# Mixer and fp4 FFN on one core: the gate projection z in eight half-length pieces, paired transpositions, decodes moved

## The chip, the cores and the metric

One core of a Trainium2 chip runs the whole kernel in one launch. The metric is the device time of one execution in microseconds. Names used below: PE is TensorE, DVE VectorE, ACT ScalarE, POOL GpSimd, SP SyncE, whose queue issues all transfers.

## The reference, cut to what matters

`x` holds 8 batches of 512 tokens of 512 features. Each layer is followed by a residual sum and a layer norm.

```python
def mixer(u, ...):                     # Mamba2-like
    z, xBC, dt = split(u @ in_proj_w.T, [1024, 1024 + 256])     # z, x: 1024; B, C: 128 each; dt: 64 heads
    x, B, C = split(silu(causal_conv4(xBC) + conv_b))
    dt = softplus(dt + dt_bias)
    y = chunked_scan(x, dt, -exp(A_log), B, C) + x * D          # chunks of 64 tokens, 64 heads of 16
    yg = y * silu(z)
    return (yg * rsqrt(mean(yg**2) + EPS) * norm_weight) @ out_proj_w.T
def ffn(x, ...):                       # weights packed as fp4 with a scale per group of 128
    h = silu(x @ w_gate.T) * (x @ w_up.T)                       # 1408 wide
    y = h @ w_down.T
    return y / sqrt(mean(y**2) + EPS)
x = layernorm(x + mixer(x)); x = layernorm(x + ffn(x))
```

## The kernel before, in words

The kernel has two phases, first the mixer for all batches, then the FFN for all. Every engine runs its own instruction stream in an order written out by hand, and they meet at semaphores (`wait_ge`, and `need`, which leaves out waits that hold anyway).

**Mixer.** After a prologue that splits `in_proj_w` into a high and a low fp16 part and projects batch 0, there is one stage `body` for each of batches 0 to 6 and a stage `last` for batch 7. A stage scans batch b in 32 slots n, chunk c = n // 4 and head group g = n % 4, while it projects batch b+1 in between: a tile of 128 columns by 512 tokens is 12 fp16 matmuls (3 passes of high and low parts over 4 row blocks) into one of two PSUM banks `ps_in`. `BODY_USES` gives the slot of each tile (dt, B, C, x0 to x7), of the fp32 out-projection of a quarter of the tokens (o0 to o3, 16 matmuls) and of its sum of squares (q0 to q3). `TAIL` and `HEAD` list what stands between slot 31 and the next scan's slot 0: I call this the border. T' is the end of q3 at a border, where the tail of one batch is done and the head of the next begins.

**A slot.** PE forms exponents in `ps_d` (`exponents`, L843), ACT takes their exponential into one of four buffers `decay` (`exp_group`, L1089), DVE multiplies two groups at a time by `gb` (`mixing`, L1381), PE applies the result within the chunk (L855). POOL scales x into `xend` (`to_end`, L1710), from which PE forms the chunk's new state (L880); `from_before` (L867) adds the older state. Once a chunk, POOL begins y with x times D (`skip_term`, L1724), and three aux groups a0, a1, a2 of PE and ACT prepare it: two of four transpositions each of `xs` (L828, taken to `xpad` by ACT, L1072), one of the product of B and C and B transposed (L831, L834, taken to `gb`, L1076). Since a `decay` buffer serves both `mixing` and `to_end`, ACT's exponentials trail both, and PE's trail ACT's:

```python
            def exp_group(b, n):
                act.wait_ge(d_full, b * SLOTS + n + 1)
                need(act, m_done, b * (SLOTS // 2) + n // 2 - 1)
                need(act, xe_done, b * SLOTS + n - 3)
```

`need(pe, e_done, b * SLOTS + n - 1)` in `exponents` is the other one. Exponential and Silu are in different tables of ACT: each change between them is an ACT_TABLE_LOAD.

**Scale of u.** fp16 splitting wants the largest |u| of a batch: DVE `measure_u` (L1259), POOL's PARTITION_ALL_REDUCE (L1700), DVE `scale_u` (L1268 to L1274), then `split_hi` on ACT (L998) and `split_lo` on DVE (L1280), and dt's matmuls (L774) are the first to read the result. `measure_u` for the batch after next stands at the border.

**Decodes.** Six units per batch of FFN weights are unpacked by DVE (`decode`, three instructions for gate/up, five for down), loaded and stored through SP.

**FFN.** Eight periods of 88 units. A full one has 176 gate/up and 132 down matmuls, fp16 128x512, down one batch behind. At four units of a period `turn` transposes a quarter of the next batch's x: four fp32 transpositions on PE (L889), ACT's high part (L1116), DVE's low part (L1485).

Of the kernel before, what the change touches and what calls it, by code (L numbers as in the profile page):

```python
# [86 lines left out]
IN_COL |= {f"z{i}": NH + 2 * NS + DI + i * P for i in range(CT)}  # L87
# [110 lines left out]
def build(nc, u_t, u_tok, w_in_t, conv_w, conv_b, dt_bias, a_log, d_skip, norm_w, w_out_t,  # L198
# [3 lines left out]
    with ctx:  # L202
# [258 lines left out]
        TURN_AT = [12 + TILE_UNITS * i for i in range(KT)]  # L461
        TILE_MMS = 3 * FT
# [1467 lines left out]
```

## Time and profile before

| | before |
|---|---|
| median of 3 runs | 1707.49 us (1706.34 to 1711.44) |
| profiled execution: time, span | 1713.24 us, 1711.1 us |
| busy PE, DVE, POOL, ACT | 92%, 76%, 64%, 53% |
| FFN's first gate/up matmul | 1140.63 us after the span's start |
| first e0 of each batch | 103.19, 223.39, 355.62, 488.82, 622.03, 755.23, 888.44, 1021.63 us |
| full FFN period | 68.22 us |

The profile is of one execution: the span is what the trace covers, 2.1 us less than that execution's time. An engine's busy share is an average over both phases. Distances between equal points of successive batches (e0 is the first `exponents` of one) are more telling than the shares.

### The profile page before, as it was taken

The numbers are of one execution on the slowest core, as the hardware profiler recorded it, in microseconds if no ns is written. First come the engines' busy times: TensorE is split into PE (matmuls) and PEld (weight loads), VectorE is DVE, ScalarE is ACT, GpSimd is POOL, SyncE is SP. The second block draws the span as 40 slices with busy tenths as digits, with TensorE's granted clock in tenths as the row PEclk, the third lists the DMA queues.
The fourth block names the chain that finished last, engine by engine and source line by source line (L and its number), as shares of the span: only waits on it lengthen the run. The fifth ranks groups of instructions, "written<-read, shape, count | busy, mean of one in ns | idle before, by whom it ended". The sixth has DMA issues, their size and how long they took to land.

```text
span 1711.1 us, 39013 instructions
## 1 busy us (share of the span) xinstructions
PE 1568.0 (92%) x14272; PEld 769.4 (45%) x14272; DVE 1301.6 (76%) x1994; ACT 906.6 (53%) x1585; POOL 1093.1 (64%) x1085
## 2 busy tenths in 40 slices
PE   2789899899999989999999997879999999999998
PEld 1245445445445445445445444433444444444443
DVE  6769859968868868868877877957777767777774
ACT  2663454364364455445545444328676756666662
POOL 0349739739729738827837845748776766767773
PEclk9899999999999999999999998989999999999999
DMA  7031161151152142133124128321010111111101
GB/s 238 8 99 31 29 142 31 29 121 50 27 115 60 23 101 64 29 79 93 27 63 111 25 55 245 51 67 38 13 62 26 62 51 34 53 44 43 35 28 62
DMA packets 214763, 109.80 MB, mean 64 GB/s; under 512 B 133876, under 2 KB 185776, under 8 KB 214576
## 3 DMA queue, kind: packets, MB, share of 16 engines
q1 hardware_dynamic: 214576, 107.37, 24.0%
q8 instruction: 109, 1.79, 0.4%
q14 instruction: 78, 0.64, 0.1%
HBM read 80.57 MB, written 26.76 MB: 63 GB/s over the span
## 4 chain that ended last, share of the span: by engine, by line
PE 69%; DVE 13%; issue 6%; ACT 6%; POOL 2%; DMA 1%; SPq 1%; DVEq 0%; ACTq 0%; POOLq 0%
PE ps_in L781 17%; PE ps_in L941 8%; PE ps_in L803 8%; PE ps_yd L956 7%; PE ps_yo L956 7%; PE ps_s L941 4%; PE ps_t L941 4%; DVE pre L1293 4%; PE ps_yd L855 3%; PE ps_yo L867 2%; PE ps_d L843 2%; PE ps_t L828 2%; PE ps_s L880 2%; ACT decay L1089 1%; ACT xpad L1072 1%
## 5 line engine op out<-in xcount | busy, mean ns | idle before, releaser
L1089 ACT ACTIVATE decay<-ps_d 128x512 f32<-128x512 f32 x256 | 149.0, 592 | 233.3 <-PE ps_d L843 179.5
L781 PE MATMUL ps_in<-u_hi,w_hi 128*128 128x512 f16 x576 | 224.3, 389 | 38.2 <-DVE pre L1293 15.9
L1710 POOL TENSOR_TENSOR xend<-xpad,decay 128x256 f32<-128x256 f32 x256 | 205.2, 822 | 69.1 <-PE ps_yo L880 47.5
L803 PE MATMUL ps_in<-w_out,zg 128*128 128x512 f32 x512 | 229.3, 601 | 0.9
L781 PE MATMUL ps_in<-u_hi,w_lo 128*128 128x512 f16 x576 | 223.6, 388 | 0.0
L781 PE MATMUL ps_in<-u_lo,w_hi 128*128 128x512 f16 x576 | 223.5, 388 | 0.0
L1818 POOL TENSOR_TENSOR gate_sum<-gate_sum,gate_part 128x512 f32<-128x512 f32 x88 | 142.1, 1615 | 104.0 <-DVE gate_part L1631 103.6
L1381 DVE TENSOR_TENSOR mix<-decay,gb 128x1024 f32<-128x1024 f32 x128 | 188.9, 1476 | 17.9 <-ACT decay L1089 16.0
L1293 DVE SCALAR_TENSOR_TENSOR pre<-ps_in,cws,pre 128x511 f32<-128x511 f32 (+2 forms) x240 | 178.9, 746 | 28.0 <-ACT pre L1029 22.3
L803 PEld LDWEIGHTS ps_in<-w_out,zg 128*128 128x128 f32 x512 | 95.5, 192 | 131.6 <-issue 131.6
L1029 ACT ACTIVATE pre<-ps_in,cb,cws 128x512 f32<-128x512 f32 x80 | 62.2, 778 | 164.2 <-PE ps_in L781 164.2
L941 PE MATMUL ps_in<-xt_hi,gu_w 128*128 128x512 f16 x352 | 134.6, 382 | 6.7 <-DVE gate_sum L1631 2.2
L941 PE MATMUL ps_in<-xt_lo,gu_w 128*128 128x512 f16 x352 | 134.4, 382 | 0.0
L1818 POOL TENSOR_TENSOR up_sum<-up_sum,up_part 128x512 f32<-128x512 f32 x88 | 112.9, 1283 | 15.9 <-DVE up_part L1631 15.5
L1724 POOL TENSOR_TENSOR y<-xs,dskip 128x512 f32<-128x512 f32 x64 | 81.2, 1269 | 58.2 <-issue 49.2
L781 PEld LDWEIGHTS ps_in<-u_hi,w_hi 128*128 128x128 f16 x576 | 57.3, 100 | 119.2 <-DVE res L1450 17.9
L843 PE MATMUL ps_d<-rhs_d,lhs_d 94*128 94x512 bf16 x256 | 102.3, 400 | 3.7 <-DMA lhs_d<-ld_dram 3.2
L1826 POOL TENSOR_TENSOR h_lo<-hf,h_hi 128x512 f16<-128x512 f32 x88 | 103.1, 1172 | 0.3 <-ACT h_hi L1222 0.3
L855 PE MATMUL ps_yd<-mix,xpad 128*32 128x64 f32 x4096 | 87.9, 229 | 14.9 <-DVE mix L1381 13.7
L1631 DVE SCALAR_TENSOR_TENSOR gate_part<-ps_in,gs,gate_part 128x512 f32<-128x512 f32 x88 | 66.0, 750 | 46.6 <-ACT gate_part L1208 36.7
L1072 ACT ACTIVATE xpad<-ps_t 64x256 f32<-64x256 f32 x256 | 95.0, 371 | 7.6 <-PE ps_t L828 6.1
L1408 DVE TENSOR_TENSOR yoff<-ps_yo,ebc 128x512 f32<-128x512 f32 x56 | 38.6, 689 | 76.8 <-PE ps_yo L867 73.4
(194 smaller groups left out, 3742.3 us busy)
## 6 DMA issues: line engine op xcount, KB each, us to landing
ebc<-e_dram SPq DMA_DIRECT2D x256, 64.0 KB, 2.8
u<-u_t SPq DMA_DIRECT2D x9, 1024.0 KB, 5.6
res<-u_tok SPq DMA_DIRECT2D x32, 256.0 KB, 3.4
x_dram<-res SPq DMA_DIRECT2D x32, 256.0 KB, 2.3
xa<-x_dram SPq DMA_DIRECT2D x8, 1024.0 KB, 6.0
xr<-x_dram SPq DMA_DIRECT2D x32, 256.0 KB, 2.6
out<-xr SPq DMA_DIRECT2D x32, 256.0 KB, 2.0
fw_words<-gu_words SPq DMA_DIRECT2D x32, 176.0 KB, 4.0
```

The lines of the kernel that those rows point to most:

```text
L781: last = mm(ps_in[bk][:, :], w[:, k, col:col + P], u[:, k, :], start=(k == 0 and j == 0), stop=(k == KT - 1 and j == 2))
L803: last = mm(ps_in[bk][:, :], zg[:, k, tt * P:(tt + 1) * P], w_out[:, k, :], start=(k == 0), stop=(k == CT - 1))
L843: mm(ps_d[n % 2][:, :].rearrange("p (k t) -> p k t", k=CT), lhs_d[0:94, c % 2, g, :], rhs_d[0:94, c % 2, g * CT:(g + 1) * CT, :], start=Tr ...
L855: last = mm(ps_yd[strip * 32:(strip + 1) * 32, tile * CH:(tile + 1) * CH], xpad[:, c % 2, g * CT + e, :], mix[:, g, e, :], start=True, sto ...
L941: last = mm(ps_gu[u % len(ps_gu)][:, :], gu_w[:, g, col:col + P], x[p.par][:, g, :], start=(j == 0), stop=(j == 1))
L956: last = mm(ps_n[tt % 2][:, :], h[par][:, k, tt * P:(tt + 1) * P], w[:, k, :], start=(step == 0), stop=(step == TILE_MMS - 1))
L1072: last = ac(xpad[rows, c % 2, 16 * use:16 * use + 16, h2 * HD:(h2 + 1) * HD], src, ACT.Copy)
L1089: ac(decay[:, n % NG, :, :].rearrange("p a b -> p (a b)"), ps_d[n % 2][:, :], ACT.Exp).then_inc(e_done, 1)
L1293: ins = v.scalar_tensor_tensor(pre[:, m, d:L], ps_in[bk][:, 0:L - d], cws[:, m, k:k + 1], pre[:, m, d:L], ALU.mult, ALU.add)
L1381: v.tensor_tensor(mix[:, g:g + 2, :, :].rearrange("p g e t -> p (g e) t"), decay[:, g:g + 2, :, :].rearrange("p g e t -> p (g e) t"), gb[: ...
L1710: g_.tensor_tensor(xend[:, pairs, :], xpad[:, c % 2, pairs, :], decay[:, g, :, CH - 1:CH].broadcast_to([P, CT, 2 * HD]), ALU.mult).then_in ...
L1818: g_.tensor_tensor(to[:, buf, :], to[:, buf, :], part[:, buf, :], ALU.add).then_inc(part_done, 1)
```

## The change

It does five things. **z** becomes eight pieces Z0 to Z7, each two column tiles by half of the tokens: 24 matmuls of 256 columns instead of 2 x 12 of 512 per pair of tiles. Z0, Z1, Z2 stand at slots 22, 24, 30 of the scan before, Z3 in place of z0, Z4 and Z5 in the border, Z6 and Z7 at slots 0 and 1. ACT takes them raw, and one Silu for each half of the tokens (`silu_z`, 128x2048) follows, at the border and at slot 12; a semaphore `z_done` tells the gates. **Transpositions** go in pairs: `xs` lies chunk by chunk, a0 is four transpositions of 128x128 with four copies to `xpad`, and with B doubled a1 is one matmul and one transposition. **Order**: `scale_u` moves from slot 0 to the end of slot 1, where it waits until Z6 and Z7 are taken; the splits, dt, B and C move a slot later; `measure_u` moves behind the last `norm_tile_end`, `take_out` ahead of `use_in`. **Decodes** of units 2 and 3 move ahead of o3's taking, units 4 and 5 to slots 2 and 3 of the next scan. **FFN**: for periods 2 to 7, x is transposed by transfers: ACT and DVE write the high and the low fp16 part (`high_half`, and `low_half` likewise on DVE, 128x512 each), SP issues eight transposing transfers of 128 KB per period, and PE waits for them at the next period's start (`xt_in`).

```diff
-DT_SLOT = {7: 0, 10: 1, 13: 2, 18: 3, 20: 4}
-SPLIT_SLOT = {1: (0, 1), 2: (2, 3)}
+DT_SLOT = {8: 0, 10: 1, 13: 2, 18: 3, 20: 4}
+SILU_Z = 12
+SPLIT_SLOT = {2: (0, 1), 3: (2, 3)}
...
-HEAD = ["a0", "z1", "z2", "e0", "a1", "e1", "z3", "a2", "e2", "z4", "z5", "z6", "z7"]
-PRO_ORDER = ["dt", "B", "C", "x0", "x1", "x2", "x3", "x4", "z0", "x5", "z1", "x6", "z2"]
-TAIL = {"pro": ["x7", "z3", "z4", "a0", "z5", "z6", "z7", "e0", "a1", "e1", "a2", "e2"], "body": ["x6", "x7", "z0", "o3", "q3"] + HEAD, "last": ["o3", "q3"]}
-AUX_ORDER = (0, 2, 1)
-NA = len(AUX_ORDER)
+HEAD = ["a0", "e0", "Z4", "a1", "e1", "Z5", "e2"]
+PRO_ORDER = ["dt", "B", "C", "x0", "x1", "x2", "x3", "x4", "Z0", "x5", "Z1", "x6", "Z4"]
+TAIL = {"pro": ["x7", "Z5", "Z2", "a0", "Z3", "e0", "a1", "e1", "e2"], "body": ["x6", "x7", "Z3", "o3", "q3"] + HEAD, "last": ["o3", "q3"]}
+NA = 2
+SILUS = 4
...
-BODY_USES = [(4, "dt"), (5, "B"), (7, "C"), (9, "x0"), (11, "x1"), (12, "o0"), (13, "q0"), (17, "x2"), (19, "x3"),
-             (20, "o1"), (21, "q1"), (25, "x4"), (27, "x5"), (28, "o2"), (29, "q2")]
-LAST_USES = [(12, "o0"), (13, "q0"), (20, "o1"), (21, "q1"), (28, "o2"), (29, "q2")]
+BODY_USES = [(0, "Z6"), (1, "Z7"), (5, "dt"), (6, "B"), (8, "C"), (9, "x0"), (11, "x1"), (12, "o0"), (13, "q0"), (17, "x2"),
+             (19, "x3"), (20, "o1"), (21, "q1"), (22, "Z0"), (24, "Z1"), (25, "x4"), (27, "x5"), (28, "o2"), (29, "q2"), (30, "Z2")]
+LAST_USES = [(0, "Z6"), (1, "Z7"), (12, "o0"), (13, "q0"), (20, "o1"), (21, "q1"), (28, "o2"), (29, "q2")]
...
-    turned = names.index("q2") + 1 if "q2" in names else len(uses)
-    return [(i + (i >= turned)) % 2 for i in range(len(uses))]
+    return [(i + sum(n in ("q1", "q2") for n in names[:i])) % 2 for i in range(len(names))]
...
-                     "last": {n: [(n // 4, n % 4)] for n in range(24)}}
-        DECODE_LATE = {"body": [2, 3, 4, 5], "last": []}
+                     "last": {n: [(n // 4 - 1, n % 4)] for n in range(4, 28)}}
+        DECODE_LATE = {"body": [2, 3], "last": []}
+        DECODE_NEXT = {2: 4, 3: 5}
...
+            def turn(f, par):
+                need(sp, gu_full, (f - 1) * UNITS)
+                settled(sp)
+                for t in range(TT):
+                    sp.wait_ge(half_hi, (f - 2) * TT + t + 1)
+                    settled(sp)
+                    sp.dma_start_transpose(xt_hi[par][:, :, t * P:(t + 1) * P], xh16[:, t, :]).then_inc(xt_in, 16)
+                    sp.wait_ge(half_lo, (f - 2) * TT + t + 1)
+                    settled(sp)
+                    sp.dma_start_transpose(xt_lo[par][:, :, t * P:(t + 1) * P], xl16[:, t, :]).then_inc(xt_in, 16)
...
+                passes = [(w_hi, u_hi), (w_hi, u_lo), (w_lo, u_hi)]
+                if name[0] == "Z":
+                    half, pair = divmod(int(name[1]), CT // 2)
+                    t = slice(half * LH, (half + 1) * LH)
+                    for i in range(2):
+                        col = Z_COL + (2 * pair + i) * P
+                        for k in range(KT):
+                            for j, (w, u) in enumerate(passes):
+                                last = mm(ps_in[bk][:, i * LH:(i + 1) * LH], w[:, k, col:col + P], u[:, k, t],
+                                          start=(k == 0 and j == 0), stop=(k == KT - 1 and j == 2))
+                    last.then_inc(in_full[bk], 1)
+                    return
...
             def aux(b, c, at):
 
-                use = AUX_ORDER[at]
                 need(pe, t_free, (b * NC + c) * NA + at)
-                t = slice(c * CH, (c + 1) * CH)
-                if use < 2:
-                    pe.wait_ge(silu_done, (b + 1) * 3)
+                if at == 0:
+                    pe.wait_ge(silu_done, b * SILUS + 2)
                     settled(pe)
-                    for k in range(4):
-                        last = tr(ps_t[0:CH, k * P:(k + 1) * P], xs[:, 4 * use + k, t], ident[:, :])
+                    for k in range(CT // 2):
+                        last = tr(ps_t[:, k * P:(k + 1) * P], xs[:, c, 2 * k * CH:2 * (k + 1) * CH], ident[:, :])
                 else:
-                    for h2 in range(2):
-                        mm(ps_t[h2 * CH:(h2 + 1) * CH, 0:CH], bc[:, 0, t], bc[:, 1, t], start=True, stop=True,
-                           tile_position=(0, h2 * CH))
-                    for h2 in range(2):
-                        last = mm(ps_t[h2 * CH:(h2 + 1) * CH, CH:CH + NS], bc[:, 0, t], ident[:, :],
-                                  start=True, stop=True, tile_position=(0, h2 * CH))
+                    pe.wait_ge(silu_done, (b + 1) * SILUS)
+                    settled(pe)
+                    mm(ps_t[:, 0:CH], b2[:, c, :], cc[:, c, :], start=True, stop=True)
+                    last = tr(ps_t[:, CH:CH + NS], b2[:, c, :], ident[:, :])
                 last.then_inc(t_full, 1)
...
             def take_z(st, name):
                 bk, _, full = st.bank(name)
                 act.wait_ge(in_full[bk], full)
...
-                if st.kind == "body" and name == "z0":
-                    ob, _, ofull = st.bank("o3")
+                if st.kind == "body" and name in ("Z0", "Z4"):
+                    ob, _, ofull = st.bank("o1" if name == "Z0" else "o3")
                     act.wait_ge(in_full[ob], ofull)
-                    act.wait_ge(sq_done, (st.scan + 1) * NC)
-                ac(zg[:, int(name[1]), :], ps_in[bk][:, :], ACT.Silu, scale=uundo[:, 0:1]).then_inc(in_free[bk], 1)
+                    act.wait_ge(sq_done, st.scan * NC + (half + 1) * NC // 2)
+                ac(zg[:, 2 * pair:2 * pair + 2, half * LH:(half + 1) * LH], ps_in[bk][:, :].rearrange("p (k t) -> p k t", k=2),
+                   ACT.Identity, scale=uundo[:, 0:1]).then_inc(in_free[bk], 1)
+
+            def silu_z(b, half):
+
+                for bk, count in Stage("last" if b == nb - 1 else "body", b).z_free(half):
+                    act.wait_ge(in_free[bk], count)
+                t = slice(half * LH, (half + 1) * LH)
+                ac(zg[:, :, t], zg[:, :, t], ACT.Silu).then_inc(z_done, 1)
...
             def aux(b, c, at):
...
+                if at == 0:
+                    need(act, yd_done, b * SLOTS + NG * (c - 1))
+                    need(act, xe_done, b * SLOTS + NG * (c - 1))
+                    for odd in range(2):
+                        for h2 in range(2):
+                            src = ps_t[odd * CH:(odd + 1) * CH, :].rearrange("p (k q h d) -> p k q h d", k=CT // 2, h=2, d=HD)
+                            dst = xpad[h2 * CH:(h2 + 1) * CH, c % 2, :, :].rearrange("p (k o q) d -> p k o q d", o=2, q=NG)
+                            last = ac(dst[:, :, odd, :, h2 * HD:(h2 + 1) * HD], src[:, :, :, h2, :], ACT.Copy)
...
-                    if n == 0 and st.proj is not None:
-                        scale_u(st.proj, st.before())
...
-                    if n > 0:
-                        use_in(st, n - 1)
                     for tt in range(TT - 1):
                         if f"o{tt}" in st.at(n - NORM_AT):
                             take_out(st, tt)
+                    if n > 0:
+                        use_in(st, n - 1)
                     if st.proj is not None:
-                        if n == 5:
+                        if n == 6:
                             dt_first(st)
                         if n in DT_SLOT:
                             dt_second(st.proj, DT_SLOT[n])
                     for k, part in DECODE_AT[st.kind].get(n, []):
                         decode(b, k, part)
+                    if b > 0 and n in DECODE_NEXT:
+                        for part in range(4):
+                            decode(b - 1, DECODE_NEXT[n], part)
+                    if n == 1 and st.proj is not None:
+                        scale_u(st.proj, st)
...
                 for tt in range(TT - 1):
                     norm_tile_end(st, tt)
-                use_in(st, SLOTS, "o")
-                if st.proj is not None:
-                    measure_u(b + 2)
-                norm_tile_end(st, TT - 1)
                 for k in DECODE_LATE[st.kind]:
                     for part in range(4):
                         decode(b, k, part)
+                use_in(st, SLOTS, "o")
+                norm_tile_end(st, TT - 1)
+                if st.proj is not None:
+                    measure_u(b + 2)
...
+            def high_half(f, t):
+                act.wait_ge(xa_in, 16 * (f + 1))
+                need(act, xt_in, (f - 2) * XT_IN)
+                ac(xh16[:, t, :], xa[:, t, :], ACT.Copy, scale=1024.0).then_inc(half_hi, 1)
```

DVE's stream at the border, before, from `measure_u` on (rows of sixteen decode instructions left out but the last; `mix` is `mixing`, `utmp` the beginning of `scale_u`, `cws` its end):

```order
L1259 TENSOR_REDUCE umax<-u 128x1
L1465 TENSOR_SCALAR res<-res,mv,rstd 128x512
...
L1372 TENSOR_TENSOR fw_lo<-fw_w,fw_hi 128x352
L1381 TENSOR_TENSOR mix<-decay,gb 128x1024
L1268 TENSOR_SCALAR utmp<-umax_all 128x1
...
L1274 TENSOR_SCALAR cws<-cw,uundo 128x40
L1381 TENSOR_TENSOR mix<-decay,gb 128x1024
L1280 SCALAR_TENSOR_TENSOR u_lo<-u,uscale,u_hi 128x512 x4
L1381 TENSOR_TENSOR mix<-decay,gb 128x1024
L1415 TENSOR_TENSOR y<-ps_yd,y 128x512
```

The same place of the changed kernel (`fw_words` to `fw_lo` is a decode of five instructions):

```order
L1535 TENSOR_SCALAR res<-res,mv,rstd 128x512
L1330 TENSOR_REDUCE umax<-u 128x1
L1452 TENSOR_TENSOR mix<-decay,gb 128x1024 x2
L1339 TENSOR_SCALAR utmp<-umax_all 128x1
...
L1351 SCALAR_TENSOR_TENSOR u_lo<-u,uscale,u_hi 128x512 x2
L1430 TENSOR_SCALAR fw_words<-fw_words,to_top 128x352
...
L1443 TENSOR_TENSOR fw_lo<-fw_mag,fw_hi 128x352
L1452 TENSOR_TENSOR mix<-decay,gb 128x1024
L1351 SCALAR_TENSOR_TENSOR u_lo<-u,uscale,u_hi 128x512 x2
```

The reduction has gone behind the last norm, the scale behind two multiplications, and a decode stands between the two halves of the split.

ACT's stream around slot 0, before (`zg` is the taking of a z tile):

```order
L1053 ACTIVATE zg<-ps_in,uundo 128x512 x5
L1089 ACT_TABLE_LOAD
L1089 ACTIVATE decay<-ps_d 128x512
L1072 ACTIVATE xpad<-ps_t 64x16x16 x2
L998 ACTIVATE u_hi<-u,uscale 128x512 x2
L1089 ACTIVATE decay<-ps_d 128x512
```

And in the changed kernel:

```order
L1154 ACTIVATE decay<-ps_d 128x512 x2
L1137 ACTIVATE xpad<-ps_t 64x4x4x16 x4
L1109 ACTIVATE zg<-ps_in,uundo 128x2x256
L1154 ACTIVATE decay<-ps_d 128x512
L1141 ACTIVATE gb<-ps_t 128x192
L1109 ACTIVATE zg<-ps_in,uundo 128x2x256
L1048 ACTIVATE u_hi<-u,uscale 128x512 x2
L1154 ACTIVATE decay<-ps_d 128x512
```

The takings of z are now among the exponentials, two of them behind the exponentials that wait for POOL, and no table is loaded between.

## Rows read from the trace of the kernel before

**Rows 1.** Windows: us, busy us of the engines (instructions), PE clock, DMA share, GB/s.

```profile
616.13:649.34 33.21, 29.78 (x229) 15.02 (x228) 22.08 (x40) 20.53 (x37) 8.86 (x12) 0.95 0.59 125
649.34:749.33 99.99, 95.37 (x1235) 48.66 (x1234) 82.58 (x116) 43.91 (x81) 78.61 (x83) 0.98 0.17 45
...
1331.37:1399.59 68.22, 68.22 (x325) 32.00 (x324) 52.09 (x88) 46.47 (x79) 48.33 (x42) 1.00 0.13 44
```

**Rows 2.** Chain of waits, one batch: start, us, piece.

```profile
520.69 0.44 PE ps_t L828 x4
...
521.35 2.59 PE ps_in L781 x12
```

**Rows 3.** Timeline of POOL at a border: start, us, instruction, idle before.

```profile
627.29 0.40 POOL L1700 PARTITION_ALL_REDUCE umax_all<-umax  x1 [7.62 <-ACT xpad L1072]
634.74 1.03 POOL L1724 TENSOR_TENSOR y<-xs,dskip 128x512 f32<-128x512 f32 x1 [7.05 <-issue]
635.74 1.79 POOL L1710 TENSOR_TENSOR xend<-xpad,decay 128x256 f32<-128x256 f32 x3
```

**Rows 4.** Waits of POOL: what for, us in total, times, longest.

```profile
POOL y L1724 <- issue: 49.2, 7, 7.2
```

**Rows 5.** Timeline of DVE at the same border.

```profile
616.17 0.16 DVE L1441 TENSOR_SCALAR msv<-ps_yo 128x1 f32<-128x1 f32 x1 [2.50 <-PE ps_yo L791]
...
618.97 2.29 DVE L1259 TENSOR_REDUCE umax<-u 128x1 f32<-128x2048 f32 x1
...
626.66 0.40 DVE L1359 TENSOR_SCALAR fw_words<-fw_words,to_top 128x352 int32<-128x352 int32 x1 [2.81 <-DMA fw_scale<-dn_scales]
...
628.48 0.53 DVE L1372 TENSOR_TENSOR fw_lo<-fw_w,fw_hi 128x352 f16<-128x352 f32 x1
...
642.02 3.52 DVE L1280 SCALAR_TENSOR_TENSOR u_lo<-u,uscale,u_hi 128x512 f16<-128x512 f32 x4
...
645.46 1.21 DVE L1381 TENSOR_TENSOR mix<-decay,gb 128x1024 f32<-128x1024 f32 x1
646.59 0.68 DVE L1415 TENSOR_TENSOR y<-ps_yd,y 128x512 f32<-128x512 f32 x1
647.20 0.69 DVE L1393 COPY state<-ps_s 128x512 f32<-128x512 f32 x1
```

**Rows 6.** Timeline of PE at the same border.

```profile
641.01 0.48 PE L831 MATMUL ps_t<-bc 128*64 128x64 f32 x4 [2.46 <-ACT xpad L1072]
...
648.85 0.34 PE L831 MATMUL ps_t<-bc 128*64 128x64 f32 x4
...
649.34 0.39 PE L781 MATMUL ps_in<-u_hi,w_hi 128*128 128x512 f16 x1
```

**Rows 7.** Timeline of ACT: at the border, and at slot 12.

```profile
638.42 1.28 ACT L1089 ACT_TABLE_LOAD   x1
...
677.83 0.60 ACT L1089 ACTIVATE decay<-ps_d 128x512 f32<-128x512 f32 x1 [7.54 <-PE ps_d L843]
```

**Rows 8.** Lines by form, ACT's Silu: busy and mean, idle before.

```profile
L1042 ACT ACTIVATE xs<-pre 128x2048 f32<-128x2048 f32 x16 | 29.6, 1894 | 0.0
```

**Rows 9.** Timelines of DVE and PE at slots 21 to 25.

```profile
706.70 0.15 DVE L1441 TENSOR_SCALAR msv<-ps_in 128x1 f32<-128x1 f32 x1
...
711.43 0.74 DVE L1450 SCALAR_TENSOR_TENSOR res<-ps_in,rinv,res 128x512 f32<-128x512 f32 x1
...
712.23 0.39 PE L781 MATMUL ps_in<-u_hi,w_hi 128*128 128x512 f16 x1 [1.81 <-DVE res L1450]
```

**Rows 10.** Timeline of PE in the last batch's scan.

```profile
1047.82 0.37 PE L867 MATMUL ps_yo<-bc,state 128*32 128x64 f32 x12
```

**Rows 11.** Lines by form, a weight load of 128 columns.

```profile
L956 PEld LDWEIGHTS ps_yd<-dn_lo,h_hi 128*128 128x128 f16 x176 | 17.3, 98 | 20.9 <-issue 0.3
```

**Rows 12.** DMA issues: times, KB each, us to landing.

```profile
xa<-x_dram SPq DMA_DIRECT2D x8, 1024.0 KB, 6.0
```

More of the change, by code:

```diff
@@ L86 @@
 IN_COL |= {f"x{i}": NH + 2 * NS + i * P for i in range(CT)}
-IN_COL |= {f"z{i}": NH + 2 * NS + DI + i * P for i in range(CT)}
+Z_COL = NH + 2 * NS + DI
+Z_HALF = [["Z0", "Z1", "Z2", "Z3"], ["Z4", "Z5", "Z6", "Z7"]]
 def need(eng, sem, value):
@@ L129, in before, with z_free @@
         return Stage("pro", 0) if isinstance(self.scan, int) and self.scan == 0 else Stage("body", self.scan - 1)
+    def z_free(self, half):
+        counts = {}
+        for name in Z_HALF[half]:
+            held = self if name in ("Z6", "Z7") else self.before()
+            bk, _, full = held.bank(name)
+            counts[bk] = max(counts.get(bk, 0), full)
+        return sorted(counts.items())
     def last_z(self):
-        found = [self.bank(f"z{i}") for i in (CT - 2, CT - 1)]
+        found = [self.bank(name) for name in ("Z6", "Z7")]
         assert found[0][0] != found[1][0]
@@ L461, in build @@
         TURN_AT = [12 + TILE_UNITS * i for i in range(KT)]
+        HALF_AT = [12 + 6 * t for t in range(TT)]
+        XT_IN = 16 * 2 * TT
         TILE_MMS = 3 * FT
@@ L614, in room_free @@
             def room_free(last):
-                for bk, full in last.before().last_z():
+                for bk, full in last.last_z():
                     sp.wait_ge(in_full[bk], full)
-                sp.wait_ge(silu_done, nb * 3)
+                sp.wait_ge(silu_done, nb * SILUS)
                 sp.wait_ge(u_max, nb + 1)
@@ L742, in ffn @@
                     load_xr(p.d, 1)
+                if p.next and not p.first:
+                    turn(p.f + 1, 1 - p.par)
                 if p.down:
@@ L970, in ffn @@
                             down(p, at)
-                    if p.next and u in TURN_AT:
+                    if p.first and u in TURN_AT:
                         turn(p.f + 1, [TURN_AT.index(u)])
@@ L989, in _, with split_hi @@
             ac = nc.scalar.activation
-            def split_hi(b, before, tiles):
+            def split_hi(b, st, tiles):
                 act.wait_ge(u_scale, (b + 1) * 5)
-                if before is not None:
-                    for bk, count in before.last_z():
+                if st is not None:
+                    for bk, count in st.last_z():
                         act.wait_ge(in_full[bk], count)
@@ L1100, in body @@
                         aux(b, c + 1, g)
+                    if n == SILU_Z:
+                        silu_z(b, 1)
                     if g == 2 and c > 0:
@@ L1103, in body @@
                     use_in(st, n)
-                    if st.proj is not None and n == 6:
+                    if st.proj is not None and n == 7:
                         exp_dt(st.proj)
@@ L1244, in ffn @@
                         squares(d, tt)
-                    if p.next and u - 2 in TURN_AT:
+                    if p.first and u - 2 in TURN_AT:
                         turn(p.f + 1, 1 - p.par, [TURN_AT.index(u - 2)])
+                    if p.next and not p.first and u - 2 in HALF_AT:
+                        high_half(p.f + 1, HALF_AT.index(u - 2))
             act.wait_ge(gs_done, 1)
@@ L1685, in ffn @@
                         normed(d, tt)
-                    if p.next and u - 5 in TURN_AT:
+                    if p.first and u - 5 in TURN_AT:
                         turn(p.f + 1, 1 - p.par, [TURN_AT.index(u - 5)])
+                    if p.next and not p.first and u - 5 in HALF_AT:
+                        low_half(p.f + 1, HALF_AT.index(u - 5))
             periods(dve, ffn)
```

138 lines of the change are left out of this document (77 added, 61 removed).

## The prediction

> **What bounds the kernel now.** I read the page's shares first: PE is busy 92% of the span, so I asked where its 8% of idle time lies and cut one batch of the mixer into two windows [rows 1]. The first runs from T' = 616.13, the end of q3, to the start of tile B at 649.34: 33.21 us with PE busy 29.78. The second, to the next T', is 99.99 us with 95.37 busy. PE sets the pace in both. A full FFN period has PE busy for all of its 68.22 us [rows 1]. So what is taken from PE is worth its length wherever PE isn't made to wait instead, and the reading to make is of the border, where the other engines have their long jobs.
>
> There POOL is the one to watch. DVE's reduction starts at 618.97 and takes 2.29 us [rows 5], so it ends at T' + 5.1. POOL's all-reduce ends at 627.69, 6.4 us later, and its next instruction, `skip_term`, starts at 634.74, after 7.05 us in which it waited for nothing that the profile names [rows 3]. That gap is there 7 times, 49.2 us in all [rows 4]. POOL is thus away from T' + 5.1 to T' + 18.6, 13.5 us, and the first `xend` stands behind it. Before, PE needs nothing of POOL in that time: it has seven z tiles of 2.6 us each [rows 2], 18 us. The 2.46 us that it waits at 641.01 [rows 6] are the first stall.
>
> **The border after, step by step** (T is the new end of q3). DVE: the decodes of units 2 and 3 fill the 2.50 us for which it waited for q3 [rows 5], so they cost nothing. The reduction now stands behind the last norm, whose 0.54 us wait for POOL's root; before, it ran meanwhile. Root ready at T + 3.5, norm to T + 4.1, reduction to T + 6.4: 1.3 us later than before. POOL is back at T + 6.4 + 13.5 = T + 19.9; `skip_term` 1.0 and the first `xend` 0.6 (1.79 for three) [rows 3] end at T + 21.5. ACT's exponential of group 4 waits for that `xend` and ends at T + 22.1.
>
> PE until then has a0 0.44, an exponent group 0.2, Z4 2.6, a1 0.3, e1 0.2, Z5 2.6, two groups 0.4, a0 of chunk 1 0.44, Z6 2.6, group 4 0.2, a1 0.3, Z7 2.6, two applications of `mix` 1.2, group 5 0.2 (2.59 and 0.44 by [rows 2]): 14.3 us. Then it stands before the exponents of group 6, which want group 4's exponential, until T + 22.1. That is a wait of 8 us in the place of z tiles that have gone elsewhere.
>
> Behind it on ACT stand `gb` and the taking of Z7 (0.3 and 0.7 [rows 7]), so Z7 is free at T + 23.1, and `scale_u`, now bound to wait for that, ends 1.25 us later at T + 24.4. The first part of `u_hi` takes 0.7: T + 25.1. DVE then has `u_lo` for two row blocks 1.8 (3.52 for four), unit 4's decode 2.35 (626.66 to 629.01), a `mix` 1.2, the other two 1.8 [rows 5]: T + 32.2. dt's 24 matmuls end 1.4 us later, T + 33.6. DVE's next row is unit 5's decode 2.35, then y 0.7 and two state copies 1.3 [rows 5], so the state is there at T + 36.5; the older state's 0.9 on PE (`from_before`) follow, and B starts at T + 37.6. Before it was 649.34 - 616.13 = T' + 33.2. **+4.4.** A decode costs nothing only where DVE waits; here each stands on the path, and without the two B would start at the later of POOL's and PE's ends, about T + 33.
>
> **From B to slot 18.** The paired transpositions save one group of 0.44 of every chunk [rows 2], and the B and C group falls from 0.49 (648.85 to 649.34 [rows 6]) to about 0.32 (64 + 128 columns, at 0.11 per transposition of 128). 0.6 a chunk is 4.8 a batch, but only the three chunks after the border and before slot 18 pass it on: **-1.8**. Those of the border fall into PE's wait, those of slots 20 to 25 before DVE's.
>
> **Slots 22 to 30.** PE's x4 at 712.23 waits for DVE's `res` of o1, after 1.81 idle; q1's mean square, which frees the bank that Z0 takes, comes at 706.70 [rows 9]. Z0 and Z1 (5.2 us) lie between these, but Z1 needs o1's bank. I put Z0 into the gap, Z1 behind `res`, and gain what the two-ahead banks give x4: +1.3, bounded by 0 (both hidden) and 5.2 - 1.8 = 3.4 (only that idle used). Z2 at slot 30 has no gap: 2.6 by [rows 2], 0.2 for its bank, **+2.8**. Batch in all: 4.4 - 1.8 + 1.3 + 2.8 = **+6.7**.
>
> **What costs nothing.** `silu_z` at slot 12 is 1.9 of Silu [rows 8] and two table loads of 1.28, 4.5 us, in ACT's idle of 7.54 before the exponential at slot 15, while PE has o0 [rows 7]. Without cover it would be up to 4.5 a batch; a 128x2048 Silu of SBUF is the same shape as the row, so I take 1.9. 256-column matmuls: a weight load takes 98 ns [rows 11], a 256-column matmul some 108 (half of 2.59 / 12), so it still hides. The bounds are nothing, and the load wholly exposed (a rival, below). Four copies to `xpad` in the place of four, of the same total, change nothing.
>
> **FFN.** 68.22 - 308 x 0.216 leaves 1.75 us of a period for 16 transpositions. They go in six periods: **-10.5**, if the transfers are in time. ACT's and DVE's halves are of the shapes of what goes. Eight transfers of 128 KB a period must land in about 55 us (the first half is ready about 15 us into a period of 68), 6.9 us each if one follows another; the nearest row lands 1024 KB in 6.0 [rows 12]. No row has a transposing transfer.
>
> The Trainium skill bears on that in "VectorE: DVE Perf Modes", section "The three transpose paths": the transposing path of DMA takes 1309 ns for 128x128 of 16 bits. By that a transfer of four blocks is an estimate of 5.2 us and a period 42 us, and the -10.5 stands; no run shown here has one.
>
> **Sum.** First batch: it has POOL's absence too, but no decodes of a batch before, so I put it at +4 from the same walk. Six more batches 6 x 6.7 = +40.2. Last batch: no projection, so no split and dt; its first `from_before` (1047.82 = T' + 32.1 [rows 10]) comes at about T + 29.5: -3. FFN -10.5. Net **+30.3** on the profiled 1713.2, 1743.5. The median of the runs is 5.7 below the profiled time: **1738**.
>
> **Rivals.**
> (a) POOL is away for only its first half. If the 7.05 us behind the all-reduce are not paid again (or not where `skip_term` is free), POOL is back at T + 12.8 [rows 3], PE never stops at group 6, and B starts 7.1 earlier, T + 30.5, 2.7 before what it was. Batch: -2.7 - 1.8 + 1.3 + 2.8 = -0.4, six times -2.4; the first -3 (+4 less 7.1), the last -5 (it has its own work on PE behind), FFN -10.5: -21, 1687. It decides once POOL's first `xend` ends before T + 14.3. For it: the profile names no cause of the gap. Against it: 7 of 7 times.
> The Trainium skill has in "GPSIMD Engine Reference", section 2.1 "Instruction dispatch", that the first call of freshly loaded code costs some 6 us. The trace has 6.4 ahead of the result, which agrees, and 7.05 again behind it, which would be the loading of the code that was there before; if only the first were such a load, (a) would hold. Chance 0.18.
> (b) PE's stalls are conserved: what waits there were stay as they are, and only PE's work counts. 4.8 x 8 = 38.4 and 10.5 less: 1658. For it: PE is busy 95.4 of 100 us behind the border. Against it: the walk. It decides if the exponents of group 6 don't wait. 0.10.
> (c) Wash: half of +6.7, by smaller waits at the border (POOL's xend in time for one decode less, Z1 hidden): 6 x 2 + 1 - 10.5 = +2.5, 1710. 0.12.
> (d) The transposing transfers are late. At 10 us each, eight take 80 of the 55: +25 in each of six periods, 150 on top of the forecast: 1888. It decides above 6.9 us each. 0.05.
> (e) Weight loads of 256-column matmuls aren't hidden: 64 pieces of 12 more matmuls of 0.1 = +77, 1815. 0.03.
> The forecast has 0.52.
>
> **The numbers.** Own range of the forecast 1722 to 1762: Z1 from 0 to 3.4 in place of 1.3 gives -8 to +13, one decode hidden -14, and the granted clock, 0.95 over the border's window [rows 1], may fall further behind the longer stop, up to +10. The whole range takes in the forecast, (a) with 12 us below it, and (c), 0.82 together, and leaves out (b), (d) and (e): 1675 to 1765. A measurement tells 0.3% (5 us) from no change. Faster: (a) and (b), 0.28. Same 0.12. Slower: the forecast, (d), (e), 0.60.
>
> **What would show it.** The chain of a batch should have POOL's `skip_term` (now about T + 19.9) and PE's exponents of group 6 idle for some 8 us with `decay` as releaser. The distance of two batches' e0 should be 139.9 in place of 133.2; B at T + 37.6; `silu_z` at slot 12 inside ACT's idle time; FFN periods of 66.5 with no PE wait at their start. It would be wrong if POOL's gap behind the all-reduce is gone, if PE doesn't reach group 6 by T + 14.3, or if DVE has its `mix` ready elsewhere than I walked.

## The result, and the profile after

The changed kernel takes 1773.78 us (median of 4 runs, 1769.59 to 1776.51), the kernel before beside it 1706.91. The ratio is 1.0375, 95% interval 1.0351 to 1.0399: slower by 67 us, where 31 were forecast. The direction was right and the size was not; the time lies outside the range. The profiled execution has a span of 1774.7 us against 1711.1, 63.6 more, and all sums below are of spans.

Part 1 of the page of the changed kernel:

```profile
PE 1533.9 (86%) x14368; PEld 825.0 (46%) x14368; DVE 1303.9 (73%) x1994; ACT 942.7 (53%) x1611; POOL 1088.9 (61%) x1085
```

PE has 34 us less to do (1568.0 us before) and is 98 us longer idle. To see where, I take the ends of q0 to q3 of each batch on PE's timeline. T is the end of q3. Means over the six intervals from the first T to the last but one, in us; first is the time to the first T, last from the seventh T to the eighth:

| kernel | T to q0 | q0 to q1 | q1 to q2 | q2 to T | batch | first | last | FFN to end |
|---|---|---|---|---|---|---|---|---|
| before | 62.6 | 24.2 | 27.8 | 18.5 | 133.0 | 217.5 | 122.8 | 570.4 |
| after | 67.3 | 23.3 | 31.5 | 21.6 | 143.6 | 225.1 | 121.8 | 564.0 |

So 6 x 10.6 = 63.5 and 7.6 at the start are lost, 1.0 and 6.4 come back. The windows of one batch (T = 656.71, tile B at 695.96, columns as in [rows 1]) and a full FFN period:

```profile
656.71:695.96 39.25, 24.88 (x316) 18.75 (x315) 20.45 (x35) 16.97 (x35) 10.98 (x14) 0.74 0.53 102
695.96:799.23 103.27, 97.08 (x1171) 53.81 (x1170) 84.89 (x121) 51.63 (x85) 76.01 (x81) 0.98 0.17 45
1331.81:1398.94 67.13, 66.83 (x309) 29.95 (x308) 52.88 (x88) 46.51 (x79) 49.30 (x42) 1.00 0.22 59
```

B starts at T + 39.25, not T' + 33.2 [rows 1], and PE is idle for 14.4 us of it instead of 3.4. The mean granted clock fell from 0.95 to 0.74 there, which is 20 us at the half level (1.2 GHz) in place of 3.4. What holds PE is on the timelines of PE, POOL, ACT and DVE:

```profile
670.31 0.39 PE L890 MATMUL ps_d<-rhs_d,lhs_d 94*128 94x512 bf16 x1
680.39 0.61 PE L890 MATMUL ps_d<-rhs_d,lhs_d 94*128 94x512 bf16 x1 [9.70 <-ACT decay L1154]
680.93 1.08 PE L902 MATMUL ps_yd<-mix,xpad 128*32 128x64 f32 x32
...
690.33 0.42 PE L825 MATMUL ps_in<-u_hi,w_hi 128*64 128x256 f16 x2 [1.41 <-issue]
...
692.65 0.45 PE L825 MATMUL ps_in<-u_hi,w_lo 128*64 128x256 f16 x2
...
751.02 0.28 PE L816 MATMUL ps_in<-u_hi,w_hi 128*128 128x256 f16 x1 [3.16 <-DVE msv L1511]
```

```profile
669.36 0.38 POOL L1781 PARTITION_ALL_REDUCE umax_all<-umax  x1 [9.09 <-issue]
678.00 1.03 POOL L1805 TENSOR_TENSOR y<-xs,dskip 128x512 f32<-128x512 f32 x1 [8.27 <-issue]
679.01 2.38 POOL L1791 TENSOR_TENSOR xend<-xpad,decay 128x256 f32<-128x256 f32 x4
```

```profile
679.74 0.60 ACT L1154 ACTIVATE decay<-ps_d 128x512 f32<-128x512 f32 x1 [12.35 <-POOL xend L1791]
680.24 0.32 ACT L1141 ACTIVATE gb<-ps_t 128x192 f32<-128x192 f32 x1
680.45 0.69 ACT L1109 ACTIVATE zg<-ps_in,uundo 128x512 f32<-128x512 f32 x1
```

```profile
660.76 2.28 DVE L1330 TENSOR_REDUCE umax<-u 128x1 f32<-128x2048 f32 x1
...
681.27 0.15 DVE L1339 TENSOR_SCALAR utmp<-umax_all 128x1 f32<-128x1 f32 x1 [15.14 <-ACT zg L1109]
...
692.33 0.52 DVE L1443 TENSOR_TENSOR fw_lo<-fw_mag,fw_hi 128x352 f16<-128x352 f32 x1
692.77 0.68 DVE L1486 TENSOR_TENSOR y<-ps_yd,y 128x512 f32<-128x512 f32 x1
```

Read them downwards in time: the reduction ends at T + 6.3, the all-reduce at T + 13.0, POOL's next instruction starts 8.27 us later at T + 21.3, the first `xend` lets ACT go on, and PE, which has stood before group 6 since T + 14.0, resumes at T + 23.7. Behind the same exponential ACT takes Z7, DVE scales, splits and decodes. DVE then works without a stop from its first `u_lo` (683.29) to the last of the two state copies (694.65), and PE waits for it at the older state, the last thing ahead of B:

```profile
694.70 1.10 PE L914 MATMUL ps_yo<-cc,state 128*32 128x64 f32 x64 [0.45 <-DVE state L1464]
```

The chain of waits of this batch goes through exactly these pieces (and has Z4 and Z0 as one piece each):

```profile
657.43 2.62 PE ps_in L816 x24
...
669.36 0.38 POOL umax_all L1781
669.73 0.07 POOLq L1805 x2
669.81 8.20 issue
678.00 1.03 POOL y L1805
679.04 0.60 POOL xend L1791
...
751.02 4.46 PE ps_in L816 x24
```

### The profile page after: what moved, and what is told of

It reads as the page before. It is cut to its first block, busy times and chain, and to the rows that moved or that the text cites. A ratio compares the mean times of both kernels' runs of the same rounds, so it can differ in the third digit from the quotient of the medians.

```text
span 1774.7 us, 39351 instructions
## 1 busy us (share of the span) xinstructions
PE 1533.9 (86%) x14368; PEld 825.0 (46%) x14368; DVE 1303.9 (73%) x1994; ACT 942.7 (53%) x1611; POOL 1088.9 (61%) x1085
## 4 chain that ended last, share of the span: by engine, by line
PE 59%; DVE 21%; issue 10%; ACT 6%; POOL 2%; DMA 1%; DVEq 0%; ACTq 0%; SPq 0%; POOLq 0%
PE ps_in L854 9%; PE ps_in L816 8%; PE ps_in L988 7%; PE ps_in L832 7%; PE ps_yd L1003 6%; PE ps_yo L1003 5%; DVE pre L1364 5%; PE ps_t L988 4%; PE ps_s L988 4%; PE ps_yd L902 2%; DVE mix L1452 2%; PE ps_yo L914 2%; PE ps_d L890 2%; PE ps_s L927 1%; DVE u_lo L1351 1%
## 5 line engine op out<-in xcount | busy, mean ns | idle before, releaser
L1791 POOL TENSOR_TENSOR xend<-xpad,decay 128x256 f32<-128x256 f32 x256 | 201.1, 808 | 77.6 <-PE ps_yo L927 41.7
L816 PE MATMUL ps_in<-u_hi,w_hi 128*128 128x256 f16 x512 | 145.6, 284 | 35.2 <-DVE msv L1511 28.2
L890 PE MATMUL ps_d<-rhs_d,lhs_d 94*128 94x512 bf16 x256 | 98.2, 410 | 84.0 <-ACT decay L1154 84.0
L816 PE MATMUL ps_in<-u_lo,w_hi 128*128 128x256 f16 x512 | 145.1, 283 | 0.0
L816 PE MATMUL ps_in<-u_hi,w_lo 128*128 128x256 f16 x512 | 145.0, 283 | 0.0
L832 PE MATMUL ps_in<-u_hi,w_hi 128*128 128x512 f16 x320 | 124.3, 388 | 20.3 <-DVE pre L1364 20.3
L1079 ACT ACTIVATE pre<-ps_in,cb,cws 128x512 f32<-128x512 f32 x80 | 62.2, 778 | 135.8 <-PE ps_in L832 135.8
L832 PE MATMUL ps_in<-u_lo,w_hi 128*128 128x512 f16 x320 | 123.8, 387 | 0.0
L832 PE MATMUL ps_in<-u_hi,w_lo 128*128 128x512 f16 x320 | 123.0, 384 | 0.0
L1109 ACT ACTIVATE zg<-ps_in,uundo 128x512 f32<-128x512 f32 x64 | 43.7, 685 | 122.9 <-PE ps_in L816 122.9
```

What stands on the lines that cost most here:

```text
L816: last = mm(ps_in[bk][:, i * LH:(i + 1) * LH], w[:, k, col:col + P], u[:, k, t], start=(k == 0 and j == 0), stop=(k == KT - 1 and j == 2))
L832: last = mm(ps_in[bk][:, :], w[:, k, col:col + P], u[:, k, :], start=(k == 0 and j == 0), stop=(k == KT - 1 and j == 2))
L890: mm(ps_d[n % 2][:, :].rearrange("p (k t) -> p k t", k=CT), lhs_d[0:94, c % 2, g, :], rhs_d[0:94, c % 2, g * CT:(g + 1) * CT, :], start=Tr ...
L1791: g_.tensor_tensor(xend[:, pairs, :], xpad[:, c % 2, pairs, :], decay[:, g, :, CH - 1:CH].broadcast_to([P, CT, 2 * HD]), ALU.mult).then_in ...
```

## The experiments

The theory (A): POOL's absence around the all-reduce stops PE at group 6, since z tiles no longer cover it, and everything that was hung behind it (the scale, two decodes, the later reduction) stands on one path; Z0 to Z2 cost their length where they went. Its rivals: the pieces, the raw taking or the pairs cost by themselves (B, C), or what was moved was hidden. Ratios are to the kernel before, with their 95% intervals; segments are in us as in the table above. The changed kernel is 64 us (0.0375 of 1710) above the kernel before; where I say how many us come back, it is the difference of two ratios times 1710. Each ratio is known to 2 to 5 us, such a difference to some 5; where it matters I give the difference of the profiled spans beside it.

**e1 and e2: no all-reduce, in the changed kernel and in the one before.** In both kernels one line of POOL:

```diff
-                g_.partition_all_reduce(umax_all[:, :], umax[:, :], P, RMAX).then_inc(u_all, 1)
+                g_.tensor_tensor(umax_all[:, :], umax[:, :], umax[:, :], ALU.mult).then_inc(u_all, 1)
```

> The changed kernel with POOL's all-reduce of umax replaced by one elementwise product, so that the largest |u| is no longer found over the partitions (the scale of u is another one; all else runs as it did). Theory A, POOL's absence around the all-reduce is what PE waits for at the exponents of group 6: POOL's skip_term starts at about T + 7 in place of T + 20.7, group 6 doesn't wait, scale_u starts at about T + 14.6 in place of T + 24.5, so each of the 7 batches with a border is some 9 to 10 us shorter (about 134 in place of 143.6) and the time falls from 1774 to about 1708. Rival B, the pieces of 256 columns, the raw eviction and the pairs themselves are what costs: the all-reduce was beside the path, and the time stays within 10 us of 1774.

> The kernel before with the same replacement. Theory A: before, seven z tiles cover POOL's absence, and scale_u waits for the last z tile and not for the all-reduce, so the time stays within 4 us of 1707. If the all-reduce costs the kernel before as much as the changed one (rival: its price is the same wherever it stands), it falls by some 60 us too.

The kernel then leaves the largest |u| over the partitions out. e1: 1704.83 us, 0.9979 (0.9956 to 1.0002). e2: 1711.1 us, 0.9999 (0.9985 to 1.0014). The same replacement takes 68 us off the changed kernel and none off the one before. T to q0 falls from 67.3 to 55.3, the other segments change by 0.6 at most. POOL's timeline of e1, where T is 622.38:

```profile
628.91 0.98 POOL L1781 TENSOR_TENSOR umax_all<-umax 128x1 f32<-128x1 f32 x1 [2.98 <-DVE umax L1330]
629.85 1.04 POOL L1805 TENSOR_TENSOR y<-xs,dskip 128x512 f32<-128x512 f32 x1
```

Both gaps around the all-reduce are gone, and PE passes group 6 at T + 13.8. PE has no wait there at all. Theory A holds for this place, and rival B, in which the all-reduce was beside the path, is refuted. The 11.3 us that come off a batch are a little more than the 10.6 that the change cost, because the border of e1 is 7.3 us shorter than that of the kernel before, while q1 to T stays 7.4 longer. So two costs stand in the changed kernel at once, PE's stop at the border and the z pieces where they went, and either one taken away alone brings back about the whole loss (e1, e3).

**e3: Z0, Z1, Z2 in the border,** and the first `silu_z` behind them.

```diff
-HEAD = ["a0", "e0", "Z4", "a1", "e1", "Z5", "e2"]
+HEAD = ["a0", "Z0", "Z1", "Z2", "e0", "Z4", "a1", "e1", "Z5", "e2"]
...
-             (19, "x3"), (20, "o1"), (21, "q1"), (22, "Z0"), (24, "Z1"), (25, "x4"), (27, "x5"), (28, "o2"), (29, "q2"), (30, "Z2")]
+             (19, "x3"), (20, "o1"), (21, "q1"), (25, "x4"), (27, "x5"), (28, "o2"), (29, "q2")]
```

> The changed kernel with Z0, Z1, Z2 moved from slots 22, 24, 30 to the border, right behind a0, and the first Silu of z behind them; no other order is changed. Theory A: they fill 7.8 of the 9.7 us for which PE waits at group 6, so the border gets no longer, while the stretch from q1 to q2 goes back from 31.6 to 28 and the one from q2 to T from 21.5 to 18.5: 6.6 us a batch, 46 in all, 1728. If PE did not really have this time free there (rival: the border gets longer by what is put in), the time stays at 1774.

1710.43 us, 0.999 (0.9973 to 1.0007): 66 us are back (62 by the spans), the whole loss, where 46 were expected. T to q0 stays at 67.2, so 7.8 us of matmuls lay free in PE's wait; PE's stop there is down to 1.23 us (0.7 to 2.2 over the seven borders):

```profile
644.08 0.39 PE L890 MATMUL ps_d<-rhs_d,lhs_d 94*128 94x512 bf16 x1 [1.23 <-ACT decay L1154]
```

q2 to T gives 3.1, as expected. q1 to q2 falls to 25.5, below the kernel before (27.8): 2.3 us that I had not counted on, which e12 explains.

**e4: the decodes of units 4 and 5 in the border.** On DVE (SP's loads and stores likewise):

```diff
-        DECODE_NEXT = {2: 4, 3: 5}
+        DECODE_NEXT = {}
...
                     measure_u(b + 2)
+                    for k in (4, 5):
+                        for part in range(4):
+                            decode(b, k, part)
```

> The changed kernel with the decodes of units 4 and 5 behind the reduction of umax in the border, where DVE idles for 15 us, in place of slots 2 and 3. Theory A: both stood on the path from scale_u to tile B (2.35 each), so B comes 4.7 us earlier (T + 34.5 in place of T + 39.2) in six batches: 28 us, 1746. Rival: POOL or ACT sets B and the decodes were hidden: no change.

1740.3 us, 1.0156 (1.0129 to 1.0183): 37 us back (32 by the spans), 28 expected. T to q0 is 62.2, 5.1 less per batch, nothing else moves. Both decodes were on the path.

**e10: the reduction of umax ahead of the last norm.** 

```diff
-                norm_tile_end(st, TT - 1)
                 if st.proj is not None:
                     measure_u(b + 2)
+                norm_tile_end(st, TT - 1)
```

> The changed kernel with only the reduction of umax back ahead of the last norm. Theory A: POOL and all that waits for it come 1.2 us earlier in each of seven borders: skip_term at T + 19.5 in place of 20.7, 142.4 us a batch, 8 us in all, 1765. Rival: DVE's takings or the root on POOL set the border, no change.

1768.32 us, 1.0327 (1.0308 to 1.0345), 8 us back; T to q0 is 66.3, 1.0 less, `skip_term` at T + 19.2 to 20.5. As expected.

**e5: all three.** e3, e4 and e10 together.

> The changed kernel with Z0, Z1, Z2 in the border as in e3, the decodes of units 4 and 5 in the border as in e4, and the reduction of umax ahead of the last norm, where it stood in the kernel before. Theory A: the three terms are on one path and add up: the batch of e3, 134.5, less 5.1 for the decodes and 1.2 for the reduction, 128.2 us a batch against 133.0 of the kernel before, some 1670 in all. Rival: with the z pieces in PE's wait, PE and not POOL sets B, and less than half of the 6.3 comes through: about 1690.

1680.95 us, 0.9822 (0.98 to 0.9844): 30 us faster than the kernel before. A batch takes 129.1 (61.3, 23.3, 26.1, 18.5) where 128.2 were expected, and the time is 11 us above the 1670 expected. By the ratios 95 us are back, and the three by themselves brought 66 + 37 + 8 = 111. Most of that difference is in the way of counting: by the spans it is 98.4 of 62.1 + 31.8 + 7.6 = 101.5, and by the batches 14.6 of 9.1 + 5.1 + 0.9 = 15.1. T to q0 gives all of its 6.0, q1 to q2 is 0.6 longer than in e3. So the three terms do add up, to about 3 us. The clock is no loss of e5 as a whole: its mean granted clock is 0.974, against 0.956, 0.950 and 0.949 in e3, e4 and e10. What the clock costs where PE sets the pace is seen within e5. Two neighbouring batches of e5, by the windows:

```profile
736.55:862.45 125.90, 116.47 (x1486) 69.36 (x1485) 105.72 (x155) 68.47 (x119) 87.76 (x94) 1.00 0.27 69
862.45:991.94 129.49, 120.45 (x1485) 71.82 (x1485) 105.37 (x155) 68.53 (x119) 87.01 (x94) 0.96 0.28 67
```

The same instructions take 3.6 us longer where the granted clock is 0.96 (10.2 us at the half level, 1.2 GHz, in its border; none in the other batch); PE's busy time grows by 4.0.

**e11: e5 without the all-reduce.** The line of e1 in e5.

> The kernel of e5 with the all-reduce replaced as in e1 (the largest |u| is not found over the partitions). In e5 PE reaches group 6 at T + 21.7 and POOL's first xend ends at T + 20.5: POOL is covered again. Theory A: at most 1.5 us a batch are left, 1670 to 1681, against the 69 that the same replacement brought the changed kernel. If POOL's absence had a second effect beside the wait at group 6 (a rival), 20 or more come off.

1684.85 us, 0.9841 (0.9825 to 0.9858), where e5 has 0.9822 (0.98 to 0.9844): nothing comes off, and the time lies above the 1670 to 1681 expected, so not even the 1.5 us a batch that I allowed for are there. PE passes group 6 at T + 21.7 in both (22.1 in one border of e5), though `xend` is ready at T + 14.6 instead of 20.3 to 21.4. Once covered, POOL's 13.5 to 14.6 us cost nothing, as in e2.

**e9: Z0 two slots later.** 

```diff
-             (19, "x3"), (20, "o1"), (21, "q1"), (22, "Z0"), (24, "Z1"), (25, "x4"), (27, "x5"), (28, "o2"), (29, "q2"), (30, "Z2")]
+             (19, "x3"), (20, "o1"), (21, "q1"), (24, "Z0"), (24, "Z1"), (25, "x4"), (27, "x5"), (28, "o2"), (29, "q2"), (30, "Z2")]
```

> The changed kernel with Z0 at slot 24 in place of 22, in front of Z1; nothing else is moved. Theory A says that Z0 costs so much at slot 22 because PE, which works in order, waits there 3.2 us for q1's mean square on DVE with the work of slots 22 and 23 behind it, and then runs Z0 at half the clock (4.5 us for 2.6). Behind that work the wait is gone or short: q1 to q2 falls from 31.5 to 28.5 to 30, 1.5 to 3 us a batch, about 1760. Rival: any 5.2 us of new work between q1 and q2 costs its length, since x4 waits for nothing any more: q1 to q2 stays at 31.5 and the time at 1774.

1766.89 us, 1.0326 (1.0309 to 1.0344), 8 us back. q1 to q2 is 30.3, 1.2 less, just short of what was expected, and 4.8 above e3's. Z0 starts without a wait of its own there and at full clock, but PE's wait has only changed its place:

```profile
743.52 0.65 PE L902 MATMUL ps_yd<-mix,xpad 128*32 128x64 f32 x32 [2.29 <-DVE mix L1452]
749.51 0.28 PE L816 MATMUL ps_in<-u_hi,w_hi 128*128 128x256 f16 x1 [0.79 <-DVE res L1520]
```

PE stands 2.29 us for DVE's `mix`, as it does in e3 without any Z there (2.28), and 0.79 before Z1. So of the 3.16 us before Z0 at slot 22 most was a wait for DVE that is there anyway. The place of Z0 was worth a fifth of the 6.0 us; the rest is that new work between q1 and q2 costs its length.

**e12: the rule of the banks alone, in the kernel before.**

```diff
-    turned = names.index("q2") + 1 if "q2" in names else len(uses)
-    return [(i + (i >= turned)) % 2 for i in range(len(uses))]
+    return [(i + sum(n in ("q1", "q2") for n in names[:i])) % 2 for i in range(len(names))]
```

> The kernel before with the changed rule of the banks alone: the order flips behind q1 too, so x4 at slot 25 takes the bank that q1's mean square frees (706.85) and not the one that the taking of o1 frees (712.17). e8 less e6 and e7 leaves it some 15 us. Theory A: the 1.8 us of idle before x4 and its half-clock stretch (1.7) go, q1 to q2 25.4 in place of 27.8, seven batches: 16 us, 1695. Rival: what follows x4 waits for DVE's taking instead (x5 takes that bank), and little or nothing is left: 1707 to 1711; the 15 us of e8 would then come of the pairs and the banks together.

1696.5 us, 0.9927 (0.9902 to 0.9951), q1 to q2 25.2 in place of 27.8 (the whole batch is 2.3 shorter). x4 no longer has the wait of 1.81 us that it has in [rows 9]:

```profile
701.34 0.55 PE L780 MATMUL ps_in<-u_hi,w_hi 128*128 128x512 f16 x1
```

A part of the change that I had not costed by itself gives 2.6 us between q1 and q2.

**e6, e7, e8: the pairs, the FFN transfers, and both with the banks, in the kernel before.** Their code is that of the change, with z, order and decodes as before. The core of e6 on PE, and of e7 on SP (e8 has both and the edit of e12):

```diff
-                    for k in range(4):
-                        last = tr(ps_t[0:CH, k * P:(k + 1) * P], xs[:, 4 * use + k, t], ident[:, :])
+                    for k in range(CT // 2):
+                        last = tr(ps_t[:, k * P:(k + 1) * P], xs[:, c, 2 * k * CH:2 * (k + 1) * CH], ident[:, :])
...
+                if p.next and not p.first:
+                    turn(p.f + 1, 1 - p.par)
```

> The kernel before with the paired transpositions alone (the layouts of xs, B and C, a0 of four and a1 of two instructions, four copies of ACT to xpad, Silu of x first); z, decodes and FFN as before. Theory A: 0.6 us of PE a chunk comes through where PE sets the pace: 0.9 from q0 to q1, some 3 us a batch, 24 in all, 1687. Rival C, four copies behind one group of transpositions are worse for ACT than two behind two: PE waits for a1 at each chunk and the time is 1707 or more.

> The kernel before with the transposing transfers of the FFN alone. The changed kernel's FFN took 564.1 us from its first matmul to the end against 570.4: 6.4 less, so 1701. The prediction's term was 10.5 (1697). Nothing in the mixer should move: 133.0 a batch.

> The kernel before with the pairs, the FFN transfers and the changed rule of the banks (the order of the two banks flips behind q1 too, so x4 takes the bank that q1 frees and not the one that o1's taking frees). In e3 that rule made q1 to q2 25.45 us in place of 27.8. Theory A: -24 for the pairs, -6.4 for the FFN, -2.35 x 7 = -16 for the banks: about 1661. If the pairs give nothing, 1685.

e6: 1702.96 us, 0.9949 (0.9931 to 0.9967), a batch 131.7, so 1.4 of its 4.8 us of PE come through, and I expected 3 (1687 in all). e7: 1704.97 us, 0.9963 (0.9953 to 0.9974), 133.0 a batch; its FFN takes 562.4 us, 8.0 less than before. e8: 1681.68 us, 0.9826 (0.9808 to 0.9844), 29.8 us; e6, e7 and e12 make 8.7 + 6.3 + 12.5 = 27.5, so the three add up as near as can be told. The 1661 expected is missed mostly by what the pairs didn't give. It is as fast as e5 (1680.95), which has z in pieces of 256 columns. That fits pieces that cost nothing, but does not show it alone: e5 also takes z raw and has the changed order and decodes.

## Why the prediction was wrong, step by step

**The border: mechanism right, +4.4 mis-sized, measured +6.0.** PE was to reach group 6 at T + 14.3 and wait until T + 22.1; it reached it at T + 14.0 and waited until T + 22.6 to 23.7. B was to start at T + 37.6 and starts, over the six borders, at T + 38.9 to 39.7, 39.4 in the mean. Half of the 1.8 missing is POOL: it is away for 14.1 to 15.0 us from the reduction's end to `skip_term`, not 13.5, because the gap behind the all-reduce is 7.2 to 8.3 where [rows 3] had 7.05, and the stretch ahead of it is up to 0.6 longer. `skip_term` is 0.9 late, and DVE's last state copy, which the walk has at T + 36.5, ends at 37.4, 0.9 late too. The other half lies behind the state copies: the older state and an exponent group, 1.1 in the walk, take 1.26 where the granted clock is back at its full level (the border shown) and up to 2.27 where it is still at half (1.2 GHz). I walked at full clock and had "up to +10" for that in the range. What the low clock does before that is beside the path: dt's 24 matmuls take 2.8 us for 1.4 in the border shown (690.33 to 693.10), and end 1.5 us before the state copies. Rival (a) is refuted: both halves of POOL's absence are paid each time. Rival (b) too, since group 6 waits.

**The decodes: right.** 4.7 by the walk, 5.1 by e4. The reduction behind the norm: 1.3 by the walk, 1.0 by e10.

**`silu_z` at slot 12: right.** It and its two table loads take 4.5 us, and ACT is idle for 2.2 more before the exponential behind them.

**From B to q1: right within 0.5.** T to q0 + q0 to q1 without the border's 6.1 is 2.3 less than before where -1.8 was put down up to slot 18.

**Slots 22 to 25: the step that failed.** I wrote "I put Z0 into the gap, Z1 behind `res`" and took +1.3 out of 0 to 3.4; measured is +3.7, beyond the bound. The step counts one idle time twice. In the kernel before, PE has 1.81 us of idle time before x4; the rest of the stretch from 706.85 to 712.23 is nearly all filled with the groups of slots 22 to 24. The bank rule, which I took together with the pieces, already uses that idle time: alone it makes q1 to q2 2.6 shorter, and x4 then waits for nothing (e12). What was left for Z0 and Z1 to hide in was nothing: they cost 31.5 - 25.5 = 6.0 us (e3), all of their 5.2 and a bit, and covered up the gain of a neighbouring edit. The bit is the place of Z0: at slot 22 it stops PE for 3.16 us and then runs at half clock (4.46 us for 2.6), which is worth 1.2 (e9). Z2: +2.8 forecast, +3.1 measured.

**FFN: mis-sized.** -10.5 forecast, -6.4 measured (e7: 6.3 by the ratio, 8.0 in its trace). 68.22 - 308 x 0.216 took the difference of two near numbers (1.69 as it is printed, not 1.75): PE's busy time of a period without transpositions is 66.8, so that they were 1.4. And PE waits 0.1 to 0.6 us in a period for DVE's sums of gate and up, which it did not before; that `low_half` ahead of them on DVE is the reason is argued, not shown. The transfers are in time, by far:

```profile
xt_hi<-xh SPq DMA_TRANSPOSE x24, 2.4
```

**The sum.** The batch is +10.6 for +6.7 (23.4 us over six), first +7.6 for +4, last -1.0 for -3, FFN 4.1 short: 33.1 more than 30.3, of 63.6 in all. Within the batch the +3.9 are 2.4 of Z0 and Z1, 1.7 of the border and 0.3 of Z2, less 0.4 from B to q1; all the others went the same way. My own range had its end at 1762, which is 1738 and the upper bounds of Z1 (13) and of the clock (10); POOL's absence, the first and the last batch and the FFN had no bound in it at all. The first batch is not the border's: it loses 5.2 from q1 to q2 and 3.1 from q2 to T and gains 0.6 ahead of them, so the +4 was missed because Z0 to Z2 stand in that batch's slots too and the walk was of the border alone. Rival (c) has a slip beside that: it calls a term "half of +6.7" and sums it as 2 a batch, where half is 3.35.

**Not settled:** why e6 passes only 1.4 of 4.8 us on. A part may be the clock: e6 has PE at the half level for 10.2 us a batch and the kernel before for 6.3, which is 2 us at most. The changed kernel has PE at the half level for 22.8 us a batch. I made no run that holds the clock fixed, so how much of its 10.6 us passes through the clock is known only for the pieces read above.

## What to carry to other kernels

Before work is moved away from a border, list the long absences of the other engines that it covers there: the seven z tiles looked like PE's load and were what hid 13.5 us of POOL. Count as a gap only what the profile calls idle there, not the distance between two events, and remember that two edits that draw on the same idle time can have it only once. Edits that touch one segment are costed apart even if they come in one diff: here a good one (2.6 us a batch) lay under a bad one (6.0). And costs that stand behind one another cannot be read off by taking one away: the all-reduce and the z pieces each seemed to be the whole loss.

## What the runs showed of the hardware

POOL pays twice for an all-reduce between ordinary instructions, every time: 6.0 to 6.7 us from the reduction's end to the all-reduce's record, and 7.2 to 8.3 behind it in the seven borders of the changed kernel (6.8 to 7.2 in the kernel before); with an elementwise instruction in its place (e1) the next one follows at once. Two all-reduces in a row pay once: at the start of the kernel before, the second follows the first without a gap (24.41 us), though its input is there since 23.0. The Trainium skill has in "GPSIMD Engine Reference", section 2.1 "Instruction dispatch", some 6 us for a first call of freshly loaded code. The rows agree with that in length ahead of the result, and have as much again behind it; that both are loads of code is not shown.

A transposing transfer of 128x512 16-bit elements lands 2.4 us after its issue (median of 48, the longest 4.8). The estimate from the Trainium skill, "VectorE: DVE Perf Modes", section "The three transpose paths", was 5.2 for four blocks; the measurement decides.

24 matmuls of 256 columns take as long as 12 of 512: 2.62 us for Z4 in the chain of waits after, 2.59 for a z tile before [rows 2]. The weight loads are hidden at 256 columns too.
